# Selective scan and two mixtures of experts on one core: layer 0's down product in float32, drive in PSUM, whole-bank scans, C rows by transfer, gathers ahead of scatters, exponentials in four lots

## The reference

```python
xn = layernorm(x)
x = x + mamba(xn) + moe0(xn)          # layer 0
xn = layernorm(x)
x = x + heads(xn) + moe1(xn)          # layer 1

# mamba: delta = softplus(xn@W_dt@W_dtproj + b); A_bar = exp(delta*A); 16 states
h[t] = A_bar[t]*h[t-1] + delta*xn*B[t];  y = sum_n C[t,n]*h[t,n] + D*xn
# moe: top 2 of 8 experts, each gelu(x@W1 + b1)@W2 + b2, hidden size 512
# heads: softmax(K)^T V over 16 heads of 8 within each token, then softmax(Q) times it
```

## Time and profile before

| | |
|---|---|
| median of 3 runs | 1028.98 us (1028.02 to 1031.87) |
| the profiled execution | 1025.65 us |
| its span, first to last instruction | 1023.9 us |
| mean granted TensorE clock | 0.816 |
| busy: TensorE, VectorE | 690.9 us (67%), 849.8 us (83%) |
| busy: ScalarE, GpSimd | 531.4 us (52%), 464.7 us (45%) |

### The profile page before, as it was taken

How to read it: one execution, slowest core, us unless ns; L and a number is a source line. 1 busy time by engine, 2 the same in 40 slices (tenths; PEclk the granted TensorE clock), 3 DMA queues, 4 the chain that set the end, 5 groups by cost and what they waited for, 6 DMA issues and landing times. The chain is left out here.

```text
span 1023.9 us, 17950 instructions
## 1 busy us (share of the span) xinstructions
PE 690.9 (67%) x4708; PEld 438.0 (43%) x4708; DVE 849.8 (83%) x1900; ACT 531.4 (52%) x1221; POOL 464.7 (45%) x451
## 2 busy tenths in 40 slices
PE   1975176787888988888882046247697697697670
PEld 0432022355354535454541036135576476475550
DVE  4899999997999999999894866846967967966967
ACT  2568422277757575858531272026755755755720
POOL 1566375544252525354421046344565465564530
PEclk9955578798999999999997555559897897897875
DMA  8241000011010101010104102000111111010108
GB/s 251 83 134 31 0 1 1 19 29 30 20 32 21 35 17 35 22 34 24 30 20 129 50 1 82 1 19 27 30 33 32 28 33 32 29 34 29 33 10 246
DMA packets 49889, 44.68 MB, mean 44 GB/s; under 512 B 8098, under 2 KB 41320, under 8 KB 49796
## 3 DMA queue, kind: packets, MB, share of 16 engines
q1 hardware_dynamic: 36356, 23.58, 7.8%
q0 software_dynamic: 9216, 17.85, 6.4%
q10 hardware_dynamic: 4224, 2.10, 0.7%
HBM read 28.82 MB, written 15.73 MB: 44 GB/s over the span
## 5 line engine op out<-in xcount | busy, mean ns | idle before, releaser
L421 POOL DMA_INDIRECT results<-res,pair_of x144 | 155.6, 1081 | 311.5 <-DVE res L1081 257.4
L415 POOL DMA_INDIRECT xrow<-rows,row_of x144 | 170.3, 1182 | 65.0 <-issue 50.7
L527 ACT ACTIVATE arena<-ph,b 128x128 f32<-128x128 f32 x432 | 123.7, 369 | 90.4 <-PE ph L723 43.7
L1120 DVE TENSOR_TENSOR_SCAN work<-decay,work 128x256 f32<-128x256 f32 x256 | 163.0, 679 | 1.1
L698 PE MATMUL py<-work,idf 128*128 128x512 f32 x256 | 140.9, 639 | 2.8 <-DVE work L1129 2.8
L519 ACT COPY xrT<-px 128x256 f16<-128x256 f16 x144 | 53.4, 371 | 169.5 <-PE px L707 131.8
L1096 DVE TENSOR_TENSOR arena<-arena 128x512 f16<-128x512 f32 x144 | 98.7, 685 | 39.5 <-ACT arena L533 37.2
L739 PE MATMUL po<-w,arena 128*128 x576 | 123.0, 293 | 0.0
L679 PE MATMUL pb<-parts,pick 96*128 96x512 bf16 x256 | 84.4, 412 | 51.5 <-DVE work L1129 39.4
L738 PE MATMUL po<-w,arena 128*128 x576 | 114.3, 233 | 0.0
L515 ACT ACTIVATE decay<-big,avec 128x512 f32<-128x512 f32 x128 | 81.7, 712 | 44.3 <-DVE work L1120 44.1
(11 more groups left out here) (196 smaller groups left out, 1545.6 us busy)
## 6 DMA issues: line engine op xcount, KB each, us to landing
decay<-in_w SPq DMA_DIRECT2D x32, 256.0 KB, 3.5
rows<-rows SPq DMA_DIRECT2D x16, 256.0 KB, 2.3
decay<-results SPq DMA_DIRECT2D x16, 256.0 KB, 3.9
big<-results SPq DMA_DIRECT2D x16, 256.0 KB, 5.0
xrow<-rows,row_of POOLq DMA_INDIRECT x144
results<-res,pair_of POOLq DMA_INDIRECT x144
x<-in_x SPq DMA_DIRECT2D x4, 512.0 KB, 6.1
out<-x ACTq DMA_DIRECT2D x8, 256.0 KB, 4.5
```

The lines of the kernel that those rows point to most:

```text
L415: e.indirect_dma_start(xrow[:, b % XR, :], None, rows_dram[l], bass.IndirectOffsetOnAxis(row_of[:, b:b + 1], 0)).then_inc(s_row[b % XR], 16)
L421: e.indirect_dma_start(res_dram[l], bass.IndirectOffsetOnAxis(pair_of[:, b:b + 1], 0), res[:, b % RR, :], None, bounds_check=NRES - 1, oob ...
L527: ins = e.activation(hid[:, b % 2, c * P:(c + 1) * P], hidden(l, b)[:, c * P:(c + 1) * P], ACT.Gelu, bias=b1[:, col(en * HC + (l * NE * HC ...
L1120: ins = e.tensor_tensor_scan(work[:, 2 + n % 2, sl], decay[:, n, sl], work[:, n % 2, sl], 0.0, ALU.mult, ALU.add)
```

## The change

- Layer 0's down product takes the gelu's float32 output and float32 weights (`w2f`, 4 transfers of 512 KB): no cast, no split, no high and low half. Layer 1 keeps the halves. The result of a block fills 128 columns of PSUM, so `block_out` is a copy; the bias comes in two products of 128 columns.
- `drive` writes back into the PSUM bank that it read (three banks in turn), and `scan` reads it there. One scan of 512 columns: `decay` is zero at the first token of each sequence (set once by GpSimd), and the exponentials leave these columns out.
- The C rows are written to DRAM in the start, and read back by SP, each row to all 128 partitions, 256 KB a step, in a ring of four. TensorE's C spread is gone; `weigh` reads SBUF. `py` is now the fourth bank of `pb`, `ph` has two banks.
- Two blocks are turned and copied at once. The up product is at lag 2, the down product at lag 4 (layer 0) or 5, the result at 5 or 6; the scatter at 6 or 7, behind the gather of block t+4. The drain has 7 ticks instead of 5.
- The ticks of a group are spread evenly over its steps (0, 7, 10, 11, 11, 11, 11, 11 a group, before 0, 9, 10, 10, 10, 11, 11, 11).
- The next group's exponentials are made in four lots of four, each followed by the table load for gelu.
- `rows` keeps two groups instead of all eight; `rows_high` waits for the transfer of the group two before.

```diff
-TICKS = ((0, 9, 10, 10, 10, 11, 11, 11), (9,) * GROUPS)
+TICKS = ((0, 7, 10, 11, 11, 11, 11, 11), (9,) * GROUPS)
+WINDOW = 4
+CR = 4
+DOWN = (4, 5)
-AHEAD = 6
+AHEAD = 4
...
+        def tick_at(g, n):
+            first = LATE if g == 1 else 0
+            here = ticks_of(0, g)
+            for i, tick in enumerate(here):
+                if n == first + (2 * i + 1) * (NS - first) // (2 * len(here)):
+                    return tick
+            return None
...
+                    for g in range(GROUPS):                      # SP
+                        for n in range(NS):
+                            at = g * NS + n
+                            if at >= CR:
+                                e.wait_ge(s_prod, at - CR + 1)
+                            e.dma_start(c_row(at), c_dram[n:n + 1, group(g)].to_broadcast([P, GC]))\
+                                .then_inc(s_c[at % CR], 16)
...
-                for b in range(BLOCKS):                          # GpSimd
-                    if b + AHEAD < BLOCKS:
-                        fetch(b + AHEAD)
-                    send(b)
+                for tick in range(BLOCKS + DRAIN):
+                    if tick + AHEAD < BLOCKS:
+                        fetch(tick + AHEAD)
+                    if (b := block_at(tick, DOWN[l] + 2)) is not None:
+                        send(b)
...
+            def rows_high(l, g):                                 # ScalarE
+                ...
+                if g >= 2:
+                    e.wait_ge(s_rout[g % 2], 16 * (g // 2 + l * GROUPS // 2))
+                e.copy(rows[:, g % 2, :, 0:D], (xf if l else xn)[:, g * TG:(g + 1) * TG, :]).then_inc(s_rhi, 1)
...
+                for n in range(NS):                              # ScalarE, scan_group
+                    if (tick := tick_at(g, n)) is not None:
+                        blocks_tick(0, tick, expert)
+                    if n % WINDOW == 0 and 0 < g * NS + n <= (GROUPS - 1) * NS:
+                        due.extend(range(g * NS + n - WINDOW, g * NS + n))
+                    if due and (tick is None or tick % 2 == 0):
+                        for at in due:
+                            decay_of(at // NS + 1, at % NS)
+                        due.clear()
+                        if g > 0:
+                            table_for(ACT.Gelu)
...
+                o = po[:, 0:D]                                   # TensorE, block_down
+                for c in range(HC if l == 0 else 0):
+                    ins = e.matmul(o, hid_f[:, b % FR, c * P:(c + 1) * P], w2f[:, bass.ds(en * HID + c * D, D)],
+                                   start=False, stop=(c == HC - 1))
...
-                e.tensor_tensor(work[:, n % 2, :], dx, pb[:, n % 2, :], ALU.mult).then_inc(s_bx, 1)
+                e.tensor_tensor(pb[:, at % 3, :], dx, pb[:, at % 3, :], ALU.mult).then_inc(s_bx, 1)
...
-                for h in range(GC // SLEN):
-                    sl = slice(h * SLEN, (h + 1) * SLEN)
-                    ins = e.tensor_tensor_scan(work[:, 2 + n % 2, sl], decay[:, n, sl], work[:, n % 2, sl],
-                                               0.0, ALU.mult, ALU.add)
+                e.tensor_tensor_scan(work[:, 2 + n % 2, :], decay[:, n, :], pb[:, at % 3, :],
+                                     0.0, ALU.mult, ALU.add).then_inc(s_scan, 1)
```

More of the change, by code:

```diff
@@ L52 @@
 POOL_HIGH = (1, 4, 6)
-assert BLOCKS >= 2 * TILES + NE - 1 and all(sum(t) == BLOCKS for t in TICKS) and BLOCKS % XR == 0 and BLOCKS % RR == 0
+assert BLOCKS >= 2 * TILES + NE - 1 and all(sum(t) == BLOCKS for t in TICKS) and BLOCKS % XR == 0 and XR % 2 == 0 and BLOCKS % RR == 0
 class Steps:
@@ L319, in _, with experts @@
                 e.dma_start(dst, src).then_inc(s_small, 16)
-            for i in range(2 * NE):
+            def experts(i):
                 l, n = i // NE, i % NE
@@ L435, in _ @@
             st = Steps(e, s_act)
[L436 to L437 removed]
+            e.sem_inc(s_v, 1)
             e.wait_ge(s_small, 16 * SMALL)
@@ L781, in scan_group @@
                         e.wait_ge(s_b2p, 1)
-                    if (i := n - (LATE if g == 1 else 0)) in range(len(ticks)):
-                        blocks_tick(0, ticks[i], expert)
+                        e.wait_ge(s_w2, 8 * NE)
+                    if (tick := tick_at(g, n)) is not None:
+                        blocks_tick(0, tick, expert)
                     if n >= 2:
```

338 lines of the change are left out of this document (189 added, 149 removed).

## The result

| | before | after |
|---|---|---|
| median (6 runs each) | 1031.03 us (1028.02 to 1035.62) | 1021.48 us (1015.58 to 1024.52) |
| ratio | | 0.9885, 95% interval 0.9848 to 0.9921 |
| profiled execution, its span | 1025.65, 1023.9 us | 1015.58, 1013.8 us |
| busy TensorE, VectorE | 690.9, 849.8 us | 699.5, 777.8 us |

Faster by 1.15% by the ratio of the runs (0.9% by the two medians), where 5% was forecast. The sign was right, the size wrong: 976 us, range 953 to 1010.

A forecast was written before the change was run, and what follows sets the result against it. VectorE was taken to pace the scan. Terms -2 (start), -62 (scan), +10 (between layers), -6 (second layer's blocks), +2 and +5 (drains) make -53: 1025.65 to 972.6, with 3.3 for the median 976 us, range 953 to 1010.

The forecast's parts named there:

- Between the layers: Before the second layer's blocks: ScalarE waits for the two-slot ring of rows; +10 us, bounds 0 and +13.
- the two drains: Ends of both layers: results come one and two ticks later; +2 us for layer 0, +5 for layer 1.
- The 2.6 us of waits a group: Scan, groups 2 to 7: VectorE's waits kept unchanged beside 41.2 us of work, giving 43.8 a group.
- Near but below: Scan: TensorE's work a group, 38.7 us or 39.9 at the granted clock, lies below VectorE's 41.2 by 1.3.
- the forecast of the scan: First layer's scan: -62 us, of which six groups 53, group 0 1 and group 1 8.
- Group 1: Scan's second group: 7 blocks instead of 9, a gain of 8 us.
- The second layer's blocks: Each result copy saves 0.12 us, VectorE setting the pace in two thirds of 72; -6, bounds -12 and +3.
- (a): Rival, scan and between the layers: waits vanish too, groups at VectorE's 41.2 us; 956 us, chance 0.13.
- (b): Rival, layer 0's down product: float32 weight loads exposed, 0.86 us a block; 1010 us, chance 0.08.
- (c): Rival, ScalarE in the scan: a table switch costs more than its load, twice 1.28 us; 1000 us, chance 0.05.
- (d): Rival, scan: the 21 added lots of exponentials are exposed as gelus bunch behind them; +58, 1034 us, chance 0.06.
- (e): Rival, scan: C row transfers set the pace, weighing waits for them; +243 us, 1219 us, chance 0.06.

The follow-up runs named there:

- e6: Changed kernel with the second layer's rows of groups 2 to 7 cast after the copies for the gate: 990.82 us, 0.9798.
- e3: Changed kernel with the scan's recurrence over 256 of the 512 columns: 974.92 us, 0.9613.
- e1: Changed kernel with TensorE's y sum moved between the tick's up product and its down product: 1004.41 us, 0.9883.
- e2: Changed kernel with half of the first layer's down product left out: 991.78 us, 0.976.
- c0: The control: the changed kernel again, no edit, on another chip than its first trace: 994.47 us, 0.9843.
- e7: Changed kernel with the head products of the second layer's first group one tick later: 993.46 us, 0.9832.
- e5: Changed kernel with the exponentials in two lots of eight a group in place of four of four: 1010.41 us, 0.9991.
- e4: Changed kernel with each C row transferred to one partition in place of 128, plus a memset of the ring: 998.45 us, 0.9839.
- e10: Changed kernel with rows of groups 2 to 7 cast late and the first group's head products one tick later: 1008.33 us, 0.9779.
- f2: Changed kernel with two scans of 256 columns in place of each of 512: 1017.61 us, 0.9945.

## Why the prediction was wrong

**Start, between the layers, drains.** Between the layers and in the two drains right, each within 2 us. The wait behind a ring of two slots was read from one row of before and came as read: 13.14 us of ScalarE, +10.3 for the stage. e6 shows it as the cause. The start's -1.5 for a forecast -2 is luck, since it doesn't stand out of that stage's scatter.

**VectorE's work in the scan.** Right: 41.6 a group against 41.2.

**The 2.6 us of waits a group.** This is the step that failed: "Keeping the 2.6 us of waits" carried before's waits over as one number. They became 3.1 us a group on a quiet chip and 5.6 in the trace of the result, whose 47.2 us are over the 47 that the prediction had named as its sign of being wrong. And they are other waits. Before, 8.9 of some 15 us in six groups were for a cast that the change removes; now 17.6 to 20.8 are for y sums. Three parts of it:
- On a quiet chip a group takes 44.8, one more than forecast. That the waits are near 2.6 there is luck; 2.0 of the 3.1 are the wait at the group's end, behind the tick of step 15. "Near but below" was not quite right for TensorE: its work is some 41.6 (e3), level with VectorE's, where the sum said 38.7 at full clock and 39.9 at the granted one.
- With late reports a group takes 47.2. That is 14.6 us of the 24 lost in the scan (5.8 more are in the six groups of the quiet trace, some 4 in group 1), and 5 us of the first group of heads (48.8 against 43.6). Late reports were in the profile of before, 27.7 us under "remote", nearly all of them on ScalarE. I neither read that row nor asked what it would do to a shorter group. The C rows are excluded as their cause by e1, e2 and c0, which have them and no late report. What holds TensorE's reports was not found, nor whether the recording of the profile takes part in it.
- So the forecast of the scan compared unlike things. From the profile used, quiet after is 53 us less (417.5 to 364.5), but that is not the change's own gain either: the medians of the same set put the whole change at 18.9 us (1013.36 to 994.47). An estimate of its gain in a quiet scan: c0's other stages are 21.6 us longer than those of the first trace of before; if late reports cost before nothing there, the scan gained 18.9 + 21.6, some 40 us of the 62.

The gain differs by set: by the medians 18.9 us on chip 5 without late reports (0.9843, 0.9813 to 0.9874), 9.6 in the first result (0.9885, 0.9848 to 0.9921) and 2.5 on chip 13 (0.9954, 0.9913 to 0.9996) with them. The first two intervals overlap, the first and the last do not. It fits that the tighter schedule suffers more: by medians of different sets the changed kernel is 25 to 27 us longer with late reports and before 8 to 19. But before differs by 10 us between two sets of chip 13 alone, so this is a reading and not shown.

**Group 1.** Forecast 42.6, measured 46.9, and 46.3 quiet. I charged before 9 blocks with all of a block's work, though by the lags only 7 splits and 5 results of its ticks fall into that group: VectorE's busy time fell by 6.1 (49.8 to 43.7), not 8. The rest is mostly 2.4 us of waits for y sums, where before had 0.6.

**The second layer's blocks.** Forecast -6, measured +10.3 in all. VectorE's busy time between the head transforms fell by 7.6 us (205.96 to 198.34), just what 0.12 a copy gives for 63 copies. The step that failed here is "in two thirds VectorE sets the pace": VectorE already waited 60 of the 268.6 us before, 37.8 of them for down products. Its longest waits before, on the same stretch, and after:

```profile
DVE res L1081 <- PE po L739: 37.8, 13, 5.9
DVE arena L1096 <- ACT arena L533: 12.7, 13, 1.9
DVE work L1259 <- PE pb L833: 4.5, 4, 1.7
```

```profile
DVE res L1159 <- PE po L819: 36.7, 16, 5.5
DVE res L1159 <- remote: 13.6, 4, 3.6
DVE work L1335 <- PE pb L912: 11.6, 7, 1.9
```

What the copies saved came back as waits, 71 us in all, for the head sums (4.5 to 11.6) among others; the quiet trace has 70 and 270.5 us. The other 7.6 us are the first group of heads. 5.2 of them are late reports: ScalarE's load for the first gelu waited for an up product that had ended at 665.08 and was reported at 669.79. In all six late traces with this order that report is 4.3 to 5.5 us late.

```profile
669.90 1.28 ACT L593 ACT_TABLE_LOAD   x1 [4.87 <-remote]
```

2.4 us are left without late reports (42.9 to 44.2 us in six quiet traces, 39.9 to 41.6 before). Here the up product stands at lag 2, behind the head products (5.19 us from 659.00, at a granted clock of 0.54), where before it stood ahead of them. This order was in the diff and I gave it no term; e7 takes 1.9 of the 2.4 back.

**The rivals.** (a) didn't come: waits grew. (b) is false as priced: eight float32 instructions with their loads take 0.99 us, where four passes of 512 columns at 0.055 us for 128 make 0.88. The loads show 0.11 a block, not 0.86. (c) is false: the exponentials start at 457.65, a load of 1.28 us at 456.36 (the earlier trace rows has the same). The Trainium skill's drain per switch (ScalarE: Activation LUTs, "What ACT_TABLE_LOAD costs") isn't in this trace: start to start, load to exponentials is 1.29 us. (d) is false for lots of four, since TensorE waits for no gelu in groups 2 to 7; e5 shows how near it is, as lots of eight cost 16 us. (e) is false: e4.

## What to carry to other kernels

When two engines have nearly the same work in a stage, the stage won't shrink by what one of them saves: here 5.4 us less for TensorE gave 0.8, 9.7 us less for VectorE gave 2.1. Take the waits of the old profile apart by releaser before carrying them over as one number: some go with the work that the change removes, others are new. Waits with no releaser in the program are worth a second trace on another chip before they go into a sum; here they were in all traces of some sets and in none of the others. And walk through the first and the last round of every loop whose order changes, with each engine's queue at hand: the last step of a group and the first group of heads each got a wait that stood in the diff.

## What the hardware showed that I had not expected

TensorE's reports to the other engines came up to 3 us late in the scan of the changed kernel, several together, and 4.3 to 5.5 us late at the first up product of the second layer. They did so at nearly the same places of the program from trace to trace: the first four remote waits behind group 2's dx stand 59.7, 76.4, 107.1 and 123.8 us after it in the first trace, and 59.8, 76.5, 107.2 and 123.9 in e10's. In the changed kernel and its variants there were 14 to 20 such bunches in 285 us in each of eight traces (the first one and seven from three later sets), and none in each of eight traces from two other sets. Between the first trace and the control they stand for 15 us in the scan and 5 in the first group of heads. VectorE and PSUM: drive writing to PSUM takes 0.686 us, as it did to SBUF (0.682), and the scan reading PSUM costs nothing more (two of 256 columns, 671 ns each in f2, 677 in before from SBUF).
